# V's pads and the selection rows set by VectorE, ScalarE and transfers, and the projections of two batches moved ahead

## The reference

```
x = L0(x)                       # non-local block: 1x1 convs, attention over pooled pixels, batch norm
x = L1(x)                       # quantized shift convolutions, batch norms, residual
t = tokens(x)                   # 8 batches x 256 tokens x 256 channels
t = t + attn(ln(t), alibi bias, causal) @ w_out + b_out      # stage 0, 16 heads of 16
t = t + ln(t) @ ternary(weight).T                            # stage 1
t = t + attn(ln(t), causal) @ w_o.T                          # stage 2, 16 heads of 16
t = t + (sum of top-2 of 8 experts, gated)(ln(t)) @ Wo.T + bo   # stage 3
out = pixels(t)
```

## Time and profile before

| | |
|---|---|
| median of 3 runs | 751.39 us (750.92 to 751.6) |
| profiled execution, its time | 752.36 us |
| its span, first to last instruction | 750.6 us |
| mean granted TensorE clock | 0.93 |
| busy: PE, PEld, DVE, ACT, POOL | 637.6, 396.0, 471.3, 320.1, 143.5 us |
| DMA queue of SP | 83176 packets, 49.81 MB |

### The profile page before, as it was taken

One profiled execution on the slowest core, in us unless ns is written; L12 is line 12 of the kernel. 1 busy time (PEld: TensorE's weight loads), 2 busy tenths in 40 slices (PEclk: granted clock), 3 DMA queues, 4 the chain that ended last, 5 costly groups with the idle time before them and its releaser, 6 DMA issues.

```text
span 750.6 us, 11202 instructions
## 1 busy us (share of the span) xinstructions
PE 637.6 (85%) x4168; PEld 396.0 (53%) x4230; DVE 471.3 (63%) x1259; ACT 320.1 (43%) x545; POOL 143.5 (19%) x126
## 2 busy tenths in 40 slices
PE   6543666349699999999999989999999999999987
PEld 3411225236366666666666655565655656564543
DVE  4777555685776776676677675737567473746433
ACT  3254554015355556555555553433434244343110
POOL 2230001572533133212203212020201100000000
PEclk9766777678799999999999999999999999999999
DMA  9300001986774995796597588246090730000000
GB/s 354 134 0 0 0 0 17 124 106 91 68 104 74 85 115 82 65 126 88 65 107 101 83 71 106 22 86 56 22 120 1 110 32 15 1 14 1 15 5 24
DMA packets 83230, 50.53 MB, mean 67 GB/s; under 512 B 4036, under 2 KB 82628, under 8 KB 82884
## 3 DMA queue, kind: packets, MB, share of 16 engines
q1 hardware_dynamic: 83176, 49.81, 46.8%
HBM read 35.11 MB, written 14.68 MB: 66 GB/s over the span
## 4 chain that ended last, share of the span: by engine, by line
PE 62%; DVE 10%; ACT 4%; issue 3%; DMA 2%; SPq 1%; POOL 0%; DVEq 0%; ACTq 0%
PE ps L1145 13%; PE ps L1031 10%; PE ps L1022 7%; PE ps L1091 4%; PE ps L1102 4%; PE ps L1087 3%; PE ps L1070 3%; PE ps L1062 3%; PE ps L1116 3%; DVE acc L1376 2%; PE ps L1014 2%; DVE nparts L1311 2%; PE ps L1156 2%; PE ps L1109 2%; PE ps L1065 2%
## 5 line engine op out<-in xcount | busy, mean ns | idle before, releaser
L1302 DVE TENSOR_REDUCE nmax<-ps 128x2 f32<-128x512 f32 (+1 forms) x192 | 130.7, 688 | 103.5 <-PE ps L1070 62.4
L1198 ACT ACTIVATE PT<-ps 128x512 f32<-128x512 f32 x192 | 114.9, 600 | 120.9 <-PE ps L1091 118.9
L1145 PE MATMUL ps<-wm,xnT 128*128 128x512 f32 x256 | 124.6, 616 | 0.6
L958 POOL TENSOR_TENSOR rstd<-ve,fix 128x2 f32<-128x2 f32 x32 | 22.2, 695 | 356.2 <-DVE ve L1264 356.2
L1192 ACT ACTIVATE QS<-ps 8x1024 bf16<-8x1024 f32 x64 | 65.1, 1017 | 40.2 <-PE ps L1075 39.4
L1376 DVE SCALAR_TENSOR_TENSOR acc<-ps,gate,acc 128x256 f32<-128x256 f32 x128 | 61.6, 481 | 29.6 <-PE ps L1145 27.3
L1091 PE MATMUL ps<-QS,KS 110*128 110x256 bf16 (+3 forms) x512 | 74.7, 248 | 0.0
L994 POOL TENSOR_TENSOR parts<-rest,fix 128x512 bf16<-128x512 f32 x30 | 38.1, 1269 | 159.9 <-DVE rest L1282 105.7
L1145 PEld LDWEIGHTS ps<-wm,xnT 128*128 128x128 f32 x256 | 45.9, 193 | 41.3 <-issue 39.0
L1022 PE MATMUL ps<-xnT,wt 128*128 128x256 f32 x256 | 65.5, 403 | 1.4 <-ACT xnT L1171 1.4
L1087 PE MATMUL ps<-fixb 128*128 128x256 bf16 (+1 forms) x192 | 60.6, 316 | 0.5 <-ACT QS L1192 0.3
(11 more groups left out here) (195 smaller groups left out, 967.9 us busy)
## 6 DMA issues: line engine op xcount, KB each, us to landing
parts_dram<-parts SPq DMA_DIRECT2D x32, 384.0 KB, 3.2
QS<-parts_dram SPq DMA_DIRECT2D x96, 128.0 KB
KS<-parts_dram SPq DMA_DIRECT2D x96, 128.0 KB, 9.8
wt<-wt_dram SPq DMA_DIRECT2D x1, 2562.0 KB, 13.1
wm<-wm_dram SPq DMA_DIRECT2D x1, 2449.0 KB, 18.4
xc<-x_dram SPq DMA_DIRECT2D x8, 256.0 KB, 5.0
out_dram<-res SPq DMA_DIRECT2D x8, 256.0 KB, 2.1
w<-w_dram SPq DMA_DIRECT2D x1, 845.0 KB, 7.4
```

The source lines that it names most:

```text
L1145: mm = pe.matmul(d, normT(stage, batch)[:, c, t * P:(t + 1) * P], M("We", c * EXPERTS * CH + e * 2 * CH, 2 * CH), start=(c == 0), stop=(c ...
L1198: act.activation(PT[:, n % PT_RING, :], bank(piece), ACT.Exp).then_inc(drain(piece), 1)
L1302: dve.tensor_reduce(group[:, 0, :] if part == 0 else group[:, 1, 2 * part - 2:2 * part], bank(piece).rearrange("p (j n) -> p j n", n=w_), ...
```

## The change

1. **PAD** no longer belongs to every batch. It is one piece of the first body, at slot -13. DVE sets V's pads of all three stacks with two memsets and adds two pieces of the identity into `chosen`, 8 x 4 values. ACT writes the selection rows of stack 0 from it in one operation of 8 x 4096. SP waits for that and copies them to stacks 1 and 2, 64 KB each. Score units wait for all of it, in the first bodies alone.
2. **V** moves from slot -10 to -14, the **LOAD**s from -11 and -10 to -12 and -11.
3. **AHEAD**: all negative slots of body 1 are 6 earlier, those of body 2 are 12 earlier. The order of TensorE at the start becomes: T, Q, K, V of batch 0; T, Q, K, V of batch 1; T, Q, K, V of batch 2; then S0 of batch 0 (before, S0 of batch 0 stood behind K of batch 1). LNa of batch 1 now stands between Q and SPLIT of batch 0 on DVE.
4. **E** moves from slots 33 to 37 and 39 to 41 to 35 to 42, CT from 43 to 44. `gate` gets a second buffer, and E on DVE waits for the gate. GB now stands ahead of the previous batch's CT.

```
 FLOW = {
     0: (("LNa", 0, 0, -21), ("LNb", 0, 0, -19), ("XB", 0, 0, -17), ("T", 0, 0, -18), ("Q", 0, 0, -16),
-        ("SPLIT", 0, 0, -15), ("K", 0, 0, -15), ("SPLIT", 0, 1, -14), ("LOAD", 0, 0, -11), ("LOAD", 0, 1, -10),
-        ("V", 0, 0, -10), ("PAD", 0, 0, -9), ("AT", 0, 0, 22), ("PR", 0, 0, 23), ("LNa", 1, 0, 24), ("LNb", 1, 0, 25),
+        ("SPLIT", 0, 0, -15), ("K", 0, 0, -15), ("SPLIT", 0, 1, -14), ("V", 0, 0, -14), ("LOAD", 0, 0, -12),
+        ("LOAD", 0, 1, -11), ("AT", 0, 0, 22), ("PR", 0, 0, 23), ("LNa", 1, 0, 24), ("LNb", 1, 0, 25),
...
-        ("SPLIT", 2, 0, -15), ("K", 2, 0, -15), ("SPLIT", 2, 1, -14), ("LOAD", 2, 0, -11), ("LOAD", 2, 1, -10),
-        ("V", 2, 0, -10), ("AT", 2, 0, 22), ("PR", 2, 0, 23),
+        ("SPLIT", 2, 0, -15), ("K", 2, 0, -15), ("SPLIT", 2, 1, -14), ("V", 2, 0, -14), ("LOAD", 2, 0, -12),
+        ("LOAD", 2, 1, -11), ("AT", 2, 0, 22), ("PR", 2, 0, 23),
...
-        ("GB", 3, 0, 32), ("E", 3, 0, 33), ("E", 3, 1, 34), ("E", 3, 2, 35), ("E", 3, 3, 36), ("E", 3, 4, 37),
-        ("E", 3, 5, 39), ("E", 3, 6, 40), ("E", 3, 7, 41), ("CT", 3, 0, 43), ("FO", 3, 0, 45)),
+        ("GB", 3, 0, 32), ("E", 3, 0, 35), ("E", 3, 1, 36), ("E", 3, 2, 37), ("E", 3, 3, 38), ("E", 3, 4, 39),
+        ("E", 3, 5, 40), ("E", 3, 6, 41), ("E", 3, 7, 42), ("CT", 3, 0, 44), ("FO", 3, 0, 45)),
 }
+AHEAD = {1: 6, 2: 12}
...
-        for k, (kind, stage, n, step) in enumerate(FLOW[s]):
+        for k, (kind, stage, n, step) in enumerate(FLOW[s] + ((("PAD", 0, 0, -13),) if at == 0 else ())):
+            if step < 0:
+                step -= AHEAD.get(at, 0)
...
+                if kind == "PAD":
+                    wait(sp, "chosen", piece)
+                    for k in range(1, STACKS):
+                        sp.dma_start(KS[MAX_AT:MAX_AT + MAX_ROWS, k], KS[MAX_AT:MAX_AT + MAX_ROWS, 0])\
+                            .then_inc(sems["chosen_spread"], 16)
...
-                if kind == "PAD" and batch < STACKS:
-                    pads = V[:, stack(stage, batch)].rearrange("p t h s -> p (t h) s")
-                    pool.memset(pads[:, :, DH + 1:], 0.0).then_inc(sems["padded"], 1)
-                    pool.memset(pads[:, :, DH:DH + 1], 1.0).then_inc(sems["padded"], 1)
...
-                    pool.tensor_tensor(KS[MAX_AT:MAX_AT + MAX_ROWS, stack(stage, batch)]
-                                       .rearrange("p (g h) n -> p g h n", h=half), *one_per_row, ALU.add)\
-                        .then_inc(sems["padded"], 1)
...
+                if kind == "PAD":
+                    wait(act, "padded", piece)
+                    one_per_row = chosen[MAX_AT:MAX_AT + MAX_ROWS, :].unsqueeze(1).unsqueeze(3)
+                    act.activation(KS[MAX_AT:MAX_AT + MAX_ROWS, 0].rearrange("p (g h) n -> p g h n", g=GROUPS),
+                                   one_per_row.broadcast_to([MAX_ROWS, GROUPS, HEADS // GROUPS, PIX]), ACT.Copy)\
+                       .then_inc(sems["chosen"], 1)
...
+                if kind == "PAD":
+                    pads = V[:].rearrange("p a t h s -> p (a t h) s")
+                    dve.memset(pads[:, :, DH + 1:], 0.0).then_inc(sems["padded"], 1)
+                    dve.memset(pads[:, :, DH:DH + 1], 1.0).then_inc(sems["padded"], 1)
+                    dve.wait_ge(fixb_loaded, 16)
...
+                    dve.tensor_tensor(chosen[rows, :], FB("ident", MAX_AT, half)[rows, :],
+                                      FB("ident", MAX_AT + half, half)[rows, :], ALU.add).then_inc(sems["padded"], 1)
...
                 if kind == "E":
                     t, e = n // 4, n % 4
+                    wait(dve, "gates_ready", ("RT", stage, batch, 3))
```

More of the change, by code:

```diff
@@ L167, in signals @@
     out += {"LNa": [("var_ready", 1), ("rstd_ready", 1)], "LNb": [("xn_ready", 1)], "XB": [("x_biased", 1)],
-            "MS": [("max_split", 1)], "PAD": [("padded", 3)] if piece[2] < STACKS else [], "FO": [("out_stored", 16)],
+            "MS": [("max_split", 1)], "PAD": [("padded", 3), ("chosen", 1), ("chosen_spread", 16 * (STACKS - 1))], "FO": [("out_stored", 16)],
             "Q": [("first_ready0", 1)], "K": [("first_ready1", 1)],
@@ L846, in build @@
             OT = lb("OT", [P, 2, PIX])
+            chosen = lb("chosen", [P, HEADS // GROUPS], BF16)
             oinv = lb("oinv", [P, 2, 2, 4])
@@ L851, in build @@
             l1 = lb("l1", [P, 3, 2])
-            gate = lb("gate", [P, 2, EXPERTS])
+            gate = lb("gate", [P, 2, 2, EXPERTS])
             gateT = lb("gateT", [EXPERTS, 2, P])
@@ L964, in pool_piece @@
                         .then_inc(sems["x_biased"], 1)
-                if kind == "PAD" and batch < STACKS:
-                    pads = V[:, stack(stage, batch)].rearrange("p t h s -> p (t h) s")
-                    done = COUNTS.after[piece, "padded"]
-                    pool.memset(pads[:, :, DH + 1:], 0.0).then_inc(sems["padded"], 1)
-                    pool.memset(pads[:, :, DH:DH + 1], 1.0).then_inc(sems["padded"], 1)
-                    pool.wait_ge(sems["padded"], done - 1)
-                    if batch == 0:
-                        pool.wait_ge(fixb_loaded, 16)
-                    chosen = FB("ident")[MAX_AT:MAX_AT + MAX_ROWS, MAX_AT:MAX_AT + MAX_ROWS]
-                    half = MAX_ROWS // PARTS_OF_MAX
-                    one_per_row = [chosen[:, r * half:(r + 1) * half].unsqueeze(1).unsqueeze(3)
-                                   .broadcast_to([MAX_ROWS, GROUPS, half, PIX]) for r in range(PARTS_OF_MAX)]
-                    pool.tensor_tensor(KS[MAX_AT:MAX_AT + MAX_ROWS, stack(stage, batch)]
-                                       .rearrange("p (g h) n -> p g h n", h=half), *one_per_row, ALU.add)\
-                        .then_inc(sems["padded"], 1)
-                    pool.wait_ge(sems["padded"], done)
                 if kind == "SPLIT" and (stage, batch) != (0, 0):
@@ L1053, in tensor_piece @@
                             pe.wait_ge(bias_loaded, 32 * STACKS)
-                        wait(pe, "padded", ("PAD", stage, batch, 0))
+                        first_body = ("PAD", *BODIES[0], 0)
+                        wait(pe, "padded", first_body)
+                        wait(pe, "chosen", first_body)
+                        if stack(stage, batch):
+                            wait(pe, "chosen_spread", first_body)
                         for k in range(2):
@@ L1133, in tensor_piece @@
                     for t in range(2):
-                        mm = pe.transpose(d[0:EXPERTS, t * P:(t + 1) * P], gate[:, t, :], F("ident"))
+                        mm = pe.transpose(d[0:EXPERTS, t * P:(t + 1) * P], gate[:, par, t, :], F("ident"))
                 if kind == "GB":
@@ L1285, in vector_piece @@
                     split(dve, piece)
+                if kind == "PAD":
[3 more added lines that the diff above has]
+                    dve.wait_ge(fixb_loaded, 16)
+                    rows = slice(MAX_AT, MAX_AT + MAX_ROWS)
+                    half = MAX_ROWS // PARTS_OF_MAX
+                    dve.tensor_tensor(chosen[rows, :], FB("ident", MAX_AT, half)[rows, :],
+                                      FB("ident", MAX_AT + half, half)[rows, :], ALU.add).then_inc(sems["padded"], 1)
                 if kind == "V":
@@ L1366, in vector_piece @@
                     settle(dve.tensor_tensor(one, one, E, ALU.mult))
-                    dve.tensor_tensor(gate[:], one, wide(m), ALU.mult).then_inc(sems["gates_ready"], 1)
+                    dve.tensor_tensor(gate[:, par], one, wide(m), ALU.mult).then_inc(sems["gates_ready"], 1)
                 if kind == "E":
                     t, e = n // 4, n % 4
+                    wait(dve, "gates_ready", ("RT", stage, batch, 3))
                     if e == 0:
@@ L1376, in vector_piece @@
                         op = dve.scalar_tensor_tensor(acc[:, t, :], bank(piece)[:, k * CH:(k + 1) * CH],
-                                                      gate[:, t, 2 * e + k:2 * e + k + 1], acc[:, t, :], ALU.mult, ALU.add)
+                                                      gate[:, par, t, 2 * e + k:2 * e + k + 1], acc[:, t, :], ALU.mult, ALU.add)
                         if k == 0:
```

## The result

The changed kernel takes **738.49 us** (median of 4 runs, 737.2 to 740.76), the kernel before 751.22 in the runs beside it: ratio 0.9829 [0.9813, 0.9845]. The forecast of 735.3 is 3.2 us too low; its range of 729.5 to 742.0 holds the result. The profiled execution took 737.2, the shortest of its four, with a span of 735.3 against 750.6.

A forecast was written before the change was run, and what follows sets the result against it. TensorE was taken as the bound, idle mainly at the start behind Pool's operations and stack loads. 9.9 + 3.8 + 2.8 - 0.4 = 16.1 us won, forecast 735.3 us, range 729.5 to 742.

The forecast's parts named there:

- Pool's PAD was the cause of the stalls: Start of attention: Pool's 7.01 us selection-row operations hold DVE, so TensorE waits 11.92, 9.53 and 6.96 us.
- Body 0's loads later: Start: statistics, pads and ACT's write delay the first load from 135.7 to 143.8, and body 0's S0 by 9 us.
- my 1.0 for the spreads: Start: the two selection-row copies ahead of body 0's loads were taken to delay them 1.0 us.
- Body 1 starts when before: Body 1's loads follow body 0's K load, so it starts at 180, before 180.4; earlier projections win nothing yet.
- Body 1's stretch: From body 1's to body 2's S0: TensorE-bound, 23.8 us plus 1.4 for half clock; body 2 at 205.3, 9.9 us won.
- V, 3.8 us: Bodies 2 to 7: V ahead of AT clears ACT's backlog and removes PR's 0.63 us wait per body, 3.8 us.
- E, 2.8 us: Bodies with experts, 430 to 690: one more E ahead of each gate wait removes 0.9 and 1.9 us, 2.8 us.
- The tail, -0.4: Last bodies: new waits for ACT copies, 4.4 us, outweigh the waits that go; net 0.4 us lost.
- Rival 1: Only the start wins; the wait at PR reappears as one for DVE; 741.9 us, chance 0.14.
- Rival 2: Body 0's loads start later still, by ACT's write or the memset and 8-engine spreads; 740.3 us, chance 0.12.
- Rival 3: More is won: faster memset, no half clock in body 1, hidden spreads, better tail; 730.2 us, chance 0.10.
- Rival 4: Slower than before: DVE becomes the bound of the E slots; 757.8 us at 1.5 us a body, chance 0.04.

The follow-up runs named there:

- fo_46: The changed kernel with FO, the last product of an expert batch, at slot 46 in place of 45; 733.85 us.
- e_back: The changed kernel with E and CT back at their slots of before (33 to 41 and 43), gate keeping two buffers; 737.4 us.
- v_back: The changed kernel with V put back by 4 slots, behind the loads, from body 3 on; 745.59 us.
- late_eback: The changed kernel with PAD at slot -10.5 in place of -13 and E and CT at their slots of before; 733.34 us.
- pad_late: The changed kernel with PAD behind the loads, at slot -10.5 in place of -13; 733.43 us.
- order_only: The changed kernel's slots, AHEAD and second gate buffer, but Pool still does PAD for each batch at slot -9; 741.08 us.
- late_fo: The changed kernel with PAD at slot -10.5 in place of -13 and FO at 46 in place of 45; 726.57 us.
- after_again: The changed kernel itself, unaltered, run again later beside other kernels; 738.66 us.
- fo_two: The changed kernel with FO at slot 46 and two DRAM buffers for split parts, one for even and one for odd bodies; 732.68 us.

## Why the prediction was right, and where it was off

- **Pool's PAD was the cause of the stalls: right.** Pool has nothing over 1.32 us after 122. One L1274, 2.01 us for its two halves, exceeds my bound of 1.1: the second took 1.31 in place of 0.41, beside Pool's L993. It cost nothing visible.
- **Body 0's loads later: right.** From the start of the phase the first QS load came at 22.1 us; I had 143.8 less 121.98, 21.8. The memset took 1.26 (I took 1.5), ACT's write 3.61 (3.6). S0 came 9.7 us later; I had 9. The right size has a wrong term in it. The load landed only 8.1 us later (39.1 after the start of the phase, 31.0 before), and S0 waited another 1.7 for TensorE's projections, which I had counted as hidden. From the first load's issue to K's landing it took 16.7 to 18.6 us (mean 17.7) in the seven executions with the spreads in front of the loads and 16.6 to 18.5 (mean 17.5) in the seven without. So my 1.0 for the spreads wasn't paid. By the rule of the Trainium skill, DMA: Bandwidth & Descriptors, section "Why a DMA increments its semaphore by 16 and not by 1", on 8 rows I had an estimate of 2.3 us, which would have made the sum 1.3 and not 1.1 us higher; such a delay isn't seen either, and how many engines carried the spreads no run here shows.
- **Body 1 starts when before: right in time, not in cause.** 58.7 and 60.6 after the start of the phase in two executions; I had 58.1. I held the load for the bound. In the first execution it was body 0's own slots, which ended 3.7 us later than worked out (58.7 against 177 less 122), and in the second the load. K's store took 4.88 us in place of the earlier trace rows's 3.2, and TensorE ran at granted 0.50 from 166 to 174. The chain of waits of the changed kernel:

```profile
148.53 10.54 DMA KS<-parts_dram
159.09 4.88 DMA parts_dram<-parts
164.05 0.84 ACT parts L1184 x2
164.92 0.87 DVE rest L1284 x2
165.79 0.66 DVE V L1307 x2
166.46 1.80 DVE nmax L1316 x3
```

- **Body 1's stretch: right.** I had 23.8, and 0 to 2.9 for the clock; it was 24.3 at clock 1.00 and 25.7 in the repeat. **9.9 us won** at body 2 was 10.2, and 6.9 in the repeat; fo_46 and e_back, whose start is the same, have 6.9 and 10.8. So 9.9 is hit in some executions and missed by 3 us in others.
- **V, 3.8 us: mechanism right.** 2.8 in the bodies 2 to 7 that I counted, 3.4 in bodies 2 to 9. I left out stage 2, where it wins 0.33 us a body with experts at their old slots and 1.20 at their new ones; v_back's 7.1 in all holds for the new ones alone.
- **E, 2.8 us: wrong.** This is the step that failed. The gate waits did go (nothing in 430 to 500). But with V at its new place the later slots took b10 to b15 from 206.7 to 202.5 and the stretch behind it from 112.1 and 115.5 up to 118.4 to 121.1: most of this was moved behind S0 of body 15 and not saved. Before, three of body 12's pieces E (slots 177 to 179) stood in front of that S0 (slot 180), now one does, and two pieces are 3.8 us of TensorE. What was saved, 0.45 us a body with experts, the new waits of the tail took back: against e_back and late_eback the medians are 1.1 and 0.1 us worse. I had counted the gate's waits at their length and overlooked that the experts at their old slots cover ACT's copy of attnT; only V's move made up for that (v_back: 45.05 a body, before 44.63).
- **The tail, -0.4: too mild.** I had listed the new waits of 0.5 to 1.3 us, and they came as listed, but no half clock behind them. E and the tail together were to win 2.4 us; from body 10 to the end it took 321.8 before and 322.2 after, with V's gain in it.
- **The sum.** 16.1 was forecast and 15.3 measured between the profiled executions, and the nearness is luck: 2.0 more from the first phase, which is chance (119.6 to 122.4 in fourteen executions), 0.3 more at the start, and 3.2 less from V, E and the tail together. In the attention phase itself it was 13.3. Between the medians on record with the profiles (751.39 and 738.49) it is 12.9: the profiled execution of before lay 1.0 above its median, that of after 1.3 below.
- **Rivals.** Rival 1 fell. TensorE has two new waits for DVE's xn in 250:430, as the row of the changed kernel below says, but not in each body, and 210.2 us for eight bodies holds V's gain in full. Rival 2 fell, since the loads started where forecast; that PAD's place in front of them costs 5.1 us (pad_late) was in my sum. Rival 3 fell on the memset's price, on the start of body 0, where the spreads were hidden but TensorE's projections were not, and on the tail; it got its 1.4 of the clock in the changed kernel and not in its repeat. Rival 4 fell: bodies with experts got shorter (43.85 from 44.63), with DVE busy 19.58 of 24.1. With V at its old slot they do get 0.42 longer (v_back), mostly by waits for ACT's copy (4.3 us in 6) and little by waits for DVE.

```profile
PE ps L1009 <- DVE xn L1274: 2.0, 2, 1.2
```

## What to carry to other kernels

A small job that is moved off a slow engine must also be placed: here it stood in front of the transfers that bound the start, and 2.5 slots later was worth 4 to 7 us. Where two chains each wait for the same copying engine, put a step of the other chain between copy and use; one slot for FO gave 4.6 us. Before a gain is read from one stretch, look where its work went: what the experts' slots won before body 15 came back behind it. Try two moves in all four combinations: V's and the experts' depend on each other. And before a buffer is added for a wait, look whether the wait is on the chain.

## What the runs showed of the hardware

- A DVE operation from SBUF to SBUF stood until Pool's 7.01 us operation on 8 partitions was done, even one of 8 elements per partition (0.17 us took 6.89); maxima read from PSUM ran beside it at their usual length (order_only, 163.60).
- The granted clock fell to 0.50 behind waits as short as 1.33 us in the tail (idle 0.47, 0.56 and 1.33 us between 701.3 and 705.3 in the changed kernel). Around 675 to 683 the waits were 0.55, 1.11 and 0.98 us, and it stayed at 1.00.
- The load of KS that starts body 1 landed 9.6 us (late_fo) to 13.0 us (after_again) after its last issue. Between the two profiled executions of the changed kernel, 735.3 and 739.5 us of span, 3.3 of the 4.2 us stand at body 2's start: 1.9 by the load and 1.4 by half clock behind it. The half clock followed in five of the eight executions in which TensorE waited for this load. fo_two, with its parts stored earlier, stayed within 2.4 us over 5 runs; that this is why was not tested.
- A DVE memset of 1,440 elements per partition took 1.26 us by its row, 0.87 ns each, with 0.25 us in front of it for which no wait is shown; ACT's 8 x 4096 copy 3.61, 0.88 ns each.
